# Layer 0 attention: scores of two heads in neighbouring PSUM banks thresholded by one instruction

## Chip, core and metric

The program runs on one core of a Trainium2 chip. The metric is the device time of one execution in microseconds (us). The core has five instruction streams: PE (TensorE, matmuls, with its weight loads listed as PEld), DVE (VectorE), ACT (ScalarE), POOL (GpSimd) and SP (SyncE, here only issuing DMAs). They meet only at semaphores. PSUM, where PE puts its results, has 8 banks of 512 fp32 columns in each of 128 partitions.

## What is computed

Two transformer layers over x of shape (2, 512, 256), each with an attention and a feed-forward part and a layer norm behind each. The change touches only the first attention, which has 16 heads of 16 channels and a threshold in place of the softmax:

```python
q, k, v = (proj(Wq), proj(Wk), proj(Wv))
scores = jnp.einsum('bhqd,bhkd->bhqk', q, k) * scale
w = jnp.where(causal, jax.nn.relu(scores - ATTN_THRESHOLD), 0.0)
w = w / (jnp.sum(w, axis=-1, keepdims=True) + EPS)
out = jnp.einsum('bhqk,bhkd->bhqd', w, v)
```

ATTN_THRESHOLD is -0.1, so every score s becomes max(s + 0.1, 0). Behind it stand layer 0's feed-forward part with Hadamard transforms, layer 1's attention with 32 query heads and a sliding window, and its feed-forward part.

## The kernel before

Everything is written out by hand: for each engine there is a list of steps (TENSOR_FIRST, SCALAR_FIRST, VECTOR_FIRST, GPSIMD_FIRST for layer 0's attention and what overlaps it), and an engine runs its steps in the order of its list. No planner decides anything, and the change leaves all lists alone.

For each of the two batches b, layer 0's 16 heads are taken in four groups hg of four heads (h4 = 0 to 3). The scores are kept transposed (128 keys in the partitions, queries in the columns), and since the mask is causal a block kb of keys needs only the queries from kb*128 on: 512, 384, 256 and 128 columns for kb = 0 to 3. A step `scores0(b, hg, part)` makes one part: part 0 is key block 0 (512 columns per head), part 1 is block 1 (384), part 2 is blocks 2 and 3 side by side (256 + 128 = 384). That is 2 x 4 x 3 = 24 steps. In each of them PE (line L553) writes four heads at the same time, each from 32 rows of the array, into four PSUM banks. Then ACT (L901) thresholds heads 0 and 2 and DVE (L1072) heads 1 and 3, one instruction per head, from PSUM into `weights_t`. POOL (L1339) waits until all four are done and zeroes the triangle of each key block with one `affine_select`. PE then multiplies by v in `pv0(b, hg, half_)` (L571; half 0 takes blocks 0 and 1, half 1 blocks 2 and 3), into bank 6. ACT copies the sums out (L911), PE turns them (L582, `turn0`, bank 7), and DVE divides (L1079 to L1081).

Six of the eight banks form a ring (RING = 6). `claim` hands out the next bank, and PE waits until the last user of that bank has emptied it: `pe.wait_ge(emptied_[bank], fills[bank])`. A `scores0` step claims four banks before its first matmul, so with six banks the next `scores0` step gets the two banks left over and the first two of the step before, when nothing else has claimed in between. The other steps that claim from the ring in this phase (`qk0`, `v0`, `at0`, `wo0`, `xt`, `prep_ug`, `prep_down`, `up`) take two banks each, so a `scores0` step always begins at an even bank.

A consumer calls `take`, which waits for the bank's `full` semaphore and returns the bank's `emptied` semaphore, to be raised by its instruction. PE's program holds an instruction's last wait in the instruction itself; the others stand ahead of it as instructions that only wait, with up to two conditions each.

## Time and profile before

| | |
|---|---|
| median of 3 runs | 520.43 us (520.12 to 520.55) |
| the profiled execution: device time | 520.81 us |
| its span, first to last instruction | 519.1 us |
| PE, DVE, ACT, POOL busy, share of the span | 92%, 74%, 65%, 46% |
| layer 0's attention, from the first scores to the last `turn0` | about 15 to 96 us |
| granted TensorE clock, mean over the span | 0.983 |

The profile is of one execution. Its page gives busy times, a line of 40 slices, the chain of work that ended last and the costliest groups; the trace behind it answers for single stretches. "Idle before <- X" names what ended an engine's idle time; a row marked x2 merges two instructions that follow each other, and its duration runs from the start of the first to the end of the second. "issue" is time in which an engine waited for nothing that the profile shows. Instructions that only wait are not listed as rows and show up as such "issue" time.

### The profile page before, as it was taken

How to read it: one execution, taken by the hardware profiler on the slowest of the kernel's cores; microseconds unless marked ns; L12 is line 12 of the kernel's file. 1: busy time of each engine (PE TensorE's matmuls, PEld its weight loads, DVE VectorE, ACT ScalarE, POOL GpSimd, SP SyncE). 2: the span in 40 equal slices, each digit the busy share in tenths (PEclk: the TensorE clock that was granted, in tenths of full speed). 3: DMA queues.
4: the chain of work that ended last, by engine and by line, in shares of the span. 5: the costliest groups of instructions: out<-in, count | busy, mean ns of one | idle time of the engine just before them, and what ended most of it. 6: DMA issues, size and time to landing. Idle time of an engine off the chain costs nothing.

```text
span 519.1 us, 10798 instructions
## 1 busy us (share of the span) xinstructions
PE 475.5 (92%) x3848; PEld 399.3 (77%) x3848; DVE 384.5 (74%) x675; ACT 335.8 (65%) x940; POOL 240.5 (46%) x167
## 2 busy tenths in 40 slices
PE   2799997999999977999999999998998699999995
PEld 1454653688888976799999999987997688889884
DVE  4455597778563689899899989999998975553534
ACT  3555564725534357998898988877988799333230
POOL 0377536321432477457656655656358821320001
PEclk9999997999999988999999999999999999999998
DMA  8500010023321000000000000001001312100101
GB/s 272 180 15 3 3 42 0 1 91 78 115 73 42 1 1 1 3 20 21 23 20 23 23 5 18 23 20 42 3 21 42 87 38 63 42 0 1 35 7 42
DMA packets 8612, 19.97 MB, mean 38 GB/s; under 512 B 1392, under 2 KB 2928, under 8 KB 8432
## 3 DMA queue, kind: packets, MB, share of 16 engines
q1 hardware_dynamic: 8560, 19.29, 11.8%
q8 instruction: 32, 0.52, 0.4%
q14 instruction: 20, 0.16, 0.1%
HBM read 18.23 MB, written 1.05 MB: 37 GB/s over the span
## 4 chain that ended last, share of the span: by engine, by line
PE 77%; DVE 11%; ACT 5%; issue 4%; DMA 1%; POOL 0%; DVEq 0%; POOLq 0%; SPq 0%; ACTq 0%
PE psum L499 17%; PE psum L501 16%; PE psum L500 15%; PE psum L553 5%; PE psum L725 4%; PE psum L715 4%; PE psum L737 4%; PE psum L571 4%; PE psum L696 3%; ACT probs L977 3%; DVE minus_max L1253 2%; PE psum L705 2%; DVE roped L1238 1%; DVE square_sums L1215 1%; DMA raw_chunks<-in_w 1%
## 5 line engine op out<-in xcount | busy, mean ns | idle before, releaser
L977 ACT ACTIVATE probs<-psum,minus_max 128x128 f32<-128x128 f32 x256 | 92.0, 399 | 16.0 <-issue 8.1
L1372 POOL TENSOR_TENSOR rope_sin_part<-qkv_rows,sin_weighted 128x640 f32<-128x640 f32 x32 | 51.2, 1623 | 48.6 <-DVE rope_cos_part L1222 42.3
L1381 POOL TENSOR_TENSOR rms_inverse<-rms_inverse,minus_half 128x20 f32<-128x20 f32 x16 | 63.5, 3970 | 1.3
L977 ACT ACTIVATION_READ_ACCUMULATOR probs<-psum,minus_max 128x1 f32 x256 | 60.7, 237 | 0.0
L945 ACT CAST hidden_high<-hidden 128x512 fp32r<-128x512 f32 x32 | 19.9, 622 | 61.1 <-DVE hidden L1168 61.1
L1253 DVE TENSOR_REDUCE minus_max<-psum 128x4 f32<-128x512 f32 x64 | 42.0, 685 | 14.6 <-PE psum L715 13.6
L499 PE MATMUL psum<-x_t_high,ug_high_low 128*128 128x512 f32 x128 | 51.1, 399 | 0.0
L501 PE MATMUL psum<-x_t_high,ug_high_low 128*128 128x512 f32 x128 | 50.7, 396 | 0.0
L500 PE MATMUL psum<-x_t_low,ug_high_low 128*128 128x512 f32 x128 | 50.5, 395 | 0.0
L499 PE MATMUL psum<-qkv_high_low,x_t_high 128*128 128x384 f32 x128 | 47.1, 368 | 3.1 <-ACT qkv_rows L950 1.7
L1247 DVE TENSOR_TENSOR probs<-probs,prob_inverse 128x512 f32<-128x512 f32 x64 | 48.0, 750 | 2.2
L950 ACT COPY qkv_rows<-psum 128x384 f32<-128x384 f32 x64 | 31.9, 511 | 18.4 <-PE psum L501 17.7
L500 PE MATMUL psum<-qkv_high_low,x_t_high 128*128 128x384 f32 x128 | 43.5, 340 | 0.0
L501 PE MATMUL psum<-qkv_high_low,x_t_low 128*128 128x384 f32 x128 | 43.4, 339 | 0.0
L1072 DVE TENSOR_SCALAR weights_t<-psum 128x384 f32<-128x384 f32 (+1 forms) x48 | 26.6, 596 | 21.2 <-PE psum L553 21.2
L901 ACT ACTIVATE weights_t<-psum,bias_threshold 128x384 f32<-128x384 f32 (+1 forms) x48 | 27.0, 616 | 22.0 <-PE psum L553 22.0
L499 PE MATMUL psum<-wout_high,out_t_high 128*128 128x256 f32 x128 | 38.7, 303 | 0.5 <-DVE out_t_low L1033 0.5
L1339 POOL TENSOR_SCALAR_AFFINE_SELECT weights_t<-weights_t 128x512 f32<-128x512 f32 x32 | 21.8, 696 | 36.8 <-DVE weights_t L1072 20.7
L1171 DVE TENSOR_TENSOR hidden_low<-hidden,hidden_high 128x512 fp32r<-128x512 f32 x32 | 22.2, 694 | 22.0 <-ACT hidden_high L945 22.0
L987 ACT COPY probs_t<-psum 128x512 f32<-128x512 f32 x64 | 37.4, 626 | 0.5 <-PE psum L725 0.3
L725 PE MATMUL psum<-identity,probs 128*128 128x128 f32 x256 | 36.2, 275 | 1.4 <-ACT probs L977 1.2
L499 PE MATMUL psum<-down_high_low,hidden_high 128*128 128x256 f32 x128 | 36.4, 284 | 0.5 <-issue 0.5
(145 smaller groups left out, 1381.4 us busy)
## 6 DMA issues: line engine op xcount, KB each, us to landing
raw_chunks<-in_ug SPq DMA_DIRECT2D x8, 512.0 KB, 3.9
raw_chunks<-in_wout SPq DMA_DIRECT2D x16, 256.0 KB, 2.8
raw_chunks<-in_qkv SPq DMA_DIRECT2D x8, 384.0 KB, 3.2
raw_chunks<-in_x SPq DMA_DIRECT2D x2, 512.0 KB, 4.6
raw_chunks<-in_w SPq DMA_DIRECT2D x2, 512.0 KB, 6.5
down_tree<-in_down SPq DMA_DIRECT2D x1, 1024.0 KB, 8.5
x_rows<-in_x_rows SPq DMA_DIRECT2D x2, 512.0 KB, 4.9
raw_chunks<-in_down SPq DMA_DIRECT2D x2, 512.0 KB, 3.9
```

What stands on the lines that cost most here:

```text
L499: nc.tensor.matmul(o, ah_, bh_, start=first, stop=False, **kw)
L500: nc.tensor.matmul(o, ah_, bl_, start=False, stop=False, **kw)
L501: return nc.tensor.matmul(o, al_, bh_, start=False, stop=last, **kw)
L725: mm = nc.tensor.transpose(o[:, q * P:(q + 1) * P], pr[:, c, q, :], ident[:])
L901: nc.scalar.activation(wt[:, hg % 2, h4, at:at + w], o[:, 0:w], ACT.Relu, bias=bias0[:]).then_inc(done, 1)
L950: nc.scalar.copy(qraw[:, k % 2, t, :], o[:, 0:GV]).then_inc(done, 1)
L977: e = nc.scalar.activation(pr[:, c, q, :], o[:, q * P:(q + 1) * P], ACT.Exp, bias=negm[:, c, q:q + 1], accum_out=psum1[:, c, q:q + 1])
L987: nc.scalar.copy(prt[:, c, :], o).then_inc(done, 1)
L1247: nc.vector.tensor_tensor(pr[:, c], pr[:, c], pinv[:, c, :].rearrange("p (q a) -> p q a", a=1).to_broadcast([P, 4, P]), ALU.mult).then_inc ...
L1253: nc.vector.tensor_reduce(negm[:, c, :], o.rearrange("p (q w) -> p q w", q=4), AX.X, ALU.max, negate=True).then_inc(mx_done[c], 1)
L1372: last = nc.gpsimd.tensor_tensor(ov[:, :, :, z, :], rv[:, :, :, 1 - z, :], sv[:, :, :, z, :], ALU.mult)
L1381: nc.gpsimd.tensor_tensor(r, r, half[:], ALU.pow).then_inc(rr_done, 1)
```

## The change

The 24 `scores0` steps claim their four banks as two pairs of neighbouring banks (0 and 1, 2 and 3, 4 and 5). A pair has a `pair_full` semaphore, raised once by each of its two heads (so the consumer waits for 2n + 2), and a `pair_emptied` semaphore, raised once by its one consumer. ACT thresholds the pair of heads 0 and 1 in one instruction over `[128, 2, w]`, DVE the pair of heads 2 and 3. POOL waits for two pair semaphores in place of four bank semaphores. Every bank now has two histories, fills as a single bank and fills as part of a pair, so every `claim` of a ring bank, up to the end of the program, waits for both. The banks that each step gets are the same as before.

```diff
@@ claim @@
                 if fills[bank]:
                     pe.wait_ge(emptied_[bank], fills[bank])
+                if bank < RING and pair_fills[bank // 2]:
+                    pe.wait_ge(pair_emptied[bank // 2], pair_fills[bank // 2])
...
+            def claim_pair(key):
+
+                if ring_at[0] % 2:
+                    ring_at[0] += 1
+                bank = ring_at[0] % RING
+                ring_at[0] += 2
+                job[key] = (bank // 2, pair_fills[bank // 2])
+                for b in (bank, bank + 1):
+                    if fills[b]:
+                        pe.wait_ge(emptied_[b], fills[b])
+                if pair_fills[bank // 2]:
+                    pe.wait_ge(pair_emptied[bank // 2], pair_fills[bank // 2])
+                pair_fills[bank // 2] += 1
+                return bank, pair_full[bank // 2]
...
-                heads = [claim(("scores0", b, hg, part, h4)) for h4 in range(HG)]
+                heads = []
+                for pr in range(2):
+                    bank, done = claim_pair(("scores0", b, hg, part, pr))
+                    heads += [(ps[:, bank + h2, :], done) for h2 in range(2)]
...
+        def take_pair(eng, key):
+
+            pair_, n = job[key]
+            eng.wait_ge(pair_full[pair_], 2 * n + 2)
+            return ps[:, 2 * pair_:2 * pair_ + 2, :], pair_emptied[pair_]
...
-                for h4 in (0, 2):
-                    o, done = take(act, ("scores0", b, hg, part, h4))
-                    nc.scalar.activation(wt[:, hg % 2, h4, at:at + w], o[:, 0:w], ACT.Relu,
-                                         bias=bias0[:]).then_inc(done, 1)
+                o, done = take_pair(act, ("scores0", b, hg, part, 0))
+                nc.scalar.activation(wt[:, hg % 2, 0:2, at:at + w], o[:, :, 0:w], ACT.Relu,
+                                     bias=bias0[:]).then_inc(done, 1)
...
-                for h4 in (1, 3):
-                    o, done = take(dve, ("scores0", b, hg, part, h4))
-                    nc.vector.tensor_scalar(wt[:, hg % 2, h4, at:at + w], o[:, 0:w], -ATTN_THRESHOLD, 0.0,
-                                            ALU.add, ALU.max).then_inc(done, 1)
+                o, done = take_pair(dve, ("scores0", b, hg, part, 1))
+                nc.vector.tensor_scalar(wt[:, hg % 2, 2:4, at:at + w], o[:, :, 0:w], -ATTN_THRESHOLD, 0.0,
+                                        ALU.add, ALU.max).then_inc(done, 1)
...
-                emptied(pool, *[("scores0", b, hg, part, h4) for h4 in range(HG)])
+                for pr in range(2):
+                    pair_, n = job["scores0", b, hg, part, pr]
+                    pool.wait_ge(pair_emptied[pair_], n + 1)
```

What stands in a row on the engines, at three places. Line numbers of the changed kernel differ: L553 has become L576, L571 L594, L499 L504, L582 L605, L901 L935, L911 L945, L885 and L887 L920 and L922.

PE at `scores0(0, 1, 0)`, `scores0(0, 1, 1)` and the first matmul of `qk0(0, 1)`, before:

```order
L553 MATMUL psum<-q_t,k_t 128x512 [waits bank5_emptied,bank0_emptied,bank4_emptied,bank1_emptied]
L553 MATMUL psum<-q_t,k_t 128x512 x3
L553 MATMUL psum<-q_t,k_t 128x384 [waits bank4_emptied,bank5_emptied,bank3_emptied,bank2_emptied]
L553 MATMUL psum<-q_t,k_t 128x384 x3
L499 MATMUL psum<-x_t_high,w_high 128x512 [waits chunk_low_dve,chunk_high,bank0_emptied]
```

The same place in the changed kernel:

```order
L576 MATMUL psum<-q_t,k_t 128x512 [waits bank0_emptied,bank1_emptied,banks45_emptied,banks01_emptied]
L576 MATMUL psum<-q_t,k_t 128x512 x3
L576 MATMUL psum<-q_t,k_t 128x384 [waits banks45_emptied,banks23_emptied]
L576 MATMUL psum<-q_t,k_t 128x384 x3
L504 MATMUL psum<-x_t_high,w_high 128x512 [waits chunk_low_dve,bank0_emptied,chunk_high,banks01_emptied]
```

No matmul has moved. The second step waited for four banks, of which 4 and 5 are heads 0 and 1 of the step right ahead; now it waits for the two pairs.

PE from `scores0(0, 1, 2)` over `pv0(0, 0, 1)` to `scores0(0, 2, 0)` and `turn0(0, 0)`, before:

```order
L553 MATMUL psum<-q_t,k_t 128x256 [waits bank4_emptied,bank5_emptied,bank3_emptied,bank2_emptied]
L553 MATMUL psum<-q_t,k_t 128x256 x3
L553 MATMUL psum<-q_t,k_t 128x128 x4
L571 MATMUL psum<-weights_t,v_and_ones 32x256 [waits weights0_masked]
L571 MATMUL psum<-weights_t,v_and_ones 32x256 x3
L571 MATMUL psum<-weights_t,v_and_ones 32x128 [waits weights0_masked]
L571 MATMUL psum<-weights_t,v_and_ones 32x128 x3
L553 MATMUL psum<-q_t,k_t 128x512 [waits bank1_emptied,bank2_emptied,bank0_emptied,bank3_emptied]
L553 MATMUL psum<-q_t,k_t 128x512 x3
L582 MATMUL psum<-identity,out_t 128x128 [waits in_identity,bank6_emptied]
```

The same place in the changed kernel:

```order
L576 MATMUL psum<-q_t,k_t 128x256 [waits banks45_emptied,banks23_emptied]
L576 MATMUL psum<-q_t,k_t 128x256 x3
L576 MATMUL psum<-q_t,k_t 128x128 x4
L594 MATMUL psum<-weights_t,v_and_ones 32x256 [waits weights0_masked]
L594 MATMUL psum<-weights_t,v_and_ones 32x256 x3
L594 MATMUL psum<-weights_t,v_and_ones 32x128 [waits weights0_masked]
L594 MATMUL psum<-weights_t,v_and_ones 32x128 x3
L576 MATMUL psum<-q_t,k_t 128x512 [waits bank1_emptied,banks01_emptied,bank0_emptied,banks23_emptied]
L576 MATMUL psum<-q_t,k_t 128x512 x3
L605 MATMUL psum<-identity,out_t 128x128 [waits in_identity,bank6_emptied]
```

Again only the waits differ: where the step waited for banks 2 and 3 apart (heads 0 and 1 of the step ahead), it waits for the pair.

ACT over the same stretch, before, with its two thresholds per step:

```order
L901 ACTIVATE weights_t<-psum,bias_threshold 128x512 [waits bank4_full,bias_set]
L901 ACTIVATE weights_t<-psum,bias_threshold 128x512 [waits bank0_full]
L901 ACTIVATE weights_t<-psum,bias_threshold 128x384 [waits bank2_full,bias_set]
L901 ACTIVATE weights_t<-psum,bias_threshold 128x384 [waits bank4_full]
L885 ACTIVATE k_t<-psum,head_parity 128x512 [waits bank0_full,in_parity]
L887 ACTIVATE q_t<-psum 128x512 [waits bank1_full]
L901 ACTIVATE weights_t<-psum,bias_threshold 128x384 [waits bank2_full,bias_set]
L901 ACTIVATE weights_t<-psum,bias_threshold 128x384 [waits bank4_full]
L911 COPY out_t<-psum 128x512 [waits bank6_full]
```

And in the changed kernel:

```order
L935 ACTIVATE weights_t<-psum,bias_threshold 128x2x512 [waits banks45_full,bias_set]
L935 ACTIVATE weights_t<-psum,bias_threshold 128x2x384 [waits banks23_full,bias_set]
L920 ACTIVATE k_t<-psum,head_parity 128x512 [waits bank0_full,in_parity]
L922 ACTIVATE q_t<-psum 128x512 [waits bank1_full]
L935 ACTIVATE weights_t<-psum,bias_threshold 128x2x384 [waits banks23_full,bias_set]
L945 COPY out_t<-psum 128x512 [waits bank6_full]
```

Two instructions of 512 or 384 columns have become one of twice as many, and nothing else on ACT has moved. DVE looks alike, with heads 2 and 3.

## Rows read from the trace of the kernel before

**Rows 1.** The page: its first line, and busy time by engine.
```profile
span 519.1 us, 10798 instructions
PE 475.5 (92%) x3848; PEld 399.3 (77%) x3848; DVE 384.5 (74%) x675; ACT 335.8 (65%) x940; POOL 240.5 (46%) x167
```
**Rows 2.** Stretches: us, busy PE, PEld, DVE, ACT, POOL (instructions), granted clock, DMA share, GB/s.
```profile
20.00:50.00 30.00, 27.41 (x276) 13.71 (x272) 16.66 (x32) 17.55 (x32) 20.39 (x20) 1.00 0.11 35
...
225.00:335.00 110.00, 110.00 (x1046) 100.56 (x1046) 100.28 (x161) 97.24 (x336) 67.62 (x37) 1.00 0.06 18
...
82.00:85.00 3.00, 0.00 (x0) 0.00 (x0) 3.00 (x8) 1.73 (x4) 1.20 (x1) 1.00 0.00 0
85.00:92.00 7.00, 6.80 (x36) 4.56 (x37) 5.18 (x13) 4.20 (x7) 5.72 (x7) 0.51 0.00 0
```
**Rows 3.** Groups by shape: line, instruction, count, busy us, mean ns, idle before, releasers.
```profile
L901 ACT ACTIVATE weights_t<-psum,bias_threshold 128x384 f32<-128x384 f32 x32 | 16.9, 581 | 11.7 <-PE psum L553 11.7
L901 ACT ACTIVATE weights_t<-psum,bias_threshold 128x512 f32<-128x512 f32 x16 | 10.1, 685 | 10.2 <-PE psum L553 10.2
L877 ACT CAST qkv_high_low<-raw_chunks 128x768 fp32r<-128x768 f32 x8 | 6.7, 832 | 0.0
L877 ACT CAST prep_high<-ug_sum_difference 128x1024 fp32r<-128x1024 f32 x4 | 4.2, 1054 | 0.0
...
L1072 DVE TENSOR_SCALAR weights_t<-psum 128x384 f32<-128x384 f32 x32 | 16.3, 552 | 11.4 <-PE psum L553 11.4
L1072 DVE TENSOR_SCALAR weights_t<-psum 128x512 f32<-128x512 f32 x16 | 10.3, 685 | 9.8 <-PE psum L553 9.8
```
**Rows 4.** The chain of waits, 24.8 to 26 us: start us, us, what.
```profile
24.91 0.70 ACT weights_t L901
25.61 0.24 issue
25.85 0.56 PE psum L553
```
**Rows 5.** Timeline at `scores0(0, 2, 0)`: start us, us, engine, line, instruction, [idle before].
```profile
30.72 1.05 ACT L901 ACTIVATE weights_t<-psum,bias_threshold 128x384 f32<-128x384 f32 x2 [0.31 <-PE psum L553]
31.55 1.14 PE L553 MATMUL psum<-q_t,k_t 32*128 32x512 f32 x8
```
**Rows 6.** Timeline at the first and the last of the alike places, `scores0(0, 0, 2)` and `scores0(1, 1, 2)`.
```profile
20.35 1.05 ACT L901 ACTIVATE weights_t<-psum,bias_threshold 128x384 f32<-128x384 f32 x2 [0.31 <-PE psum L553]
21.18 0.94 PE L553 MATMUL psum<-q_t,k_t 32*128 32x256 f32 x16 [0.91 <-ACT weights_t L901]
...
62.73 1.05 ACT L901 ACTIVATE weights_t<-psum,bias_threshold 128x384 f32<-128x384 f32 x2 [1.82 <-PE psum L553]
63.56 0.71 PE L553 MATMUL psum<-q_t,k_t 32*128 32x256 f32 x8
```
**Rows 7.** Timeline at the last two `scores0` steps, 83.7 to 88 us.
```profile
83.77 1.28 DVE L1072 TENSOR_SCALAR weights_t<-psum 128x512 f32<-128x512 f32 x2
85.19 1.61 PE L553 MATMUL psum<-q_t,k_t 32*128 32x384 f32 x5 [3.22 <-DVE weights_t L1072]
...
86.91 1.05 ACT L901 ACTIVATE weights_t<-psum,bias_threshold 128x384 f32<-128x384 f32 x2 [0.97 <-PE psum L553]
87.83 1.67 PE L553 MATMUL psum<-q_t,k_t 32*128 32x256 f32 x16
```
**Rows 8.** PE behind POOL's masks: total of such idle time; two rows at 80 us.
```profile
  POOL weights_t L1339: 2.0, 5
...
80.21 1.28 POOL L1339 TENSOR_SCALAR_AFFINE_SELECT weights_t<-weights_t 128x512 f32<-128x512 f32 x2
...
81.55 0.16 PEld L571 LDWEIGHTS psum<-weights_t,v_and_ones 128*32 128x32 f32 x8 [0.48 <-POOL weights_t L1339]
```
**Rows 9.** PE's waits from 95 us on, largest and smallest group: total us, times, longest.
```profile
PE psum L696 <- DVE roped L1238: 2.9, 1, 2.9
...
PE psum L499 <- ACT probs_t L987: 0.4, 1, 0.4
```

More of the change, by code:

```diff
@@ L414, in post_ln_two_layers @@
         emptied_ = [sem(f"bank{i}_emptied") for i in range(8)]
+        pair_full = [sem(f"banks{2 * i}{2 * i + 1}_full") for i in range(RING // 2)]
+        pair_emptied = [sem(f"banks{2 * i}{2 * i + 1}_emptied") for i in range(RING // 2)]
         ch_in = [sem(f"chunk_in{i}") for i in range(SLOTS)]
@@ L450, in post_ln_two_layers @@
         fills = [0] * 8
+        pair_fills = [0] * (RING // 2)
         ring_at = [0]
@@ L783, in take, with pair_filled @@
             return ps[:, bank, :], emptied_[bank]
+        def pair_filled(eng, key):
+            pair_, n = job[key]
+            eng.wait_ge(pair_full[pair_], 2 * n + 2)
+        def take_pair(eng, key):
+            pair_, n = job[key]
+            eng.wait_ge(pair_full[pair_], 2 * n + 2)
+            return ps[:, 2 * pair_:2 * pair_ + 2, :], pair_emptied[pair_]
         def filled(eng, key):
@@ L881, in qk0 @@
                 if b:
-                    filled(act, ("scores0", b - 1, 2 * m + 1, 2, HG - 1))
+                    for pr in range(2):
+                        pair_filled(act, ("scores0", b - 1, 2 * m + 1, 2, pr))
                 o, _ = take(act, ("qk0", b, 1, m))
@@ L1062, in qk0 @@
                 if b:
-                    filled(dve, ("scores0", b - 1, 2 * m + 1, 2, HG - 1))
+                    for pr in range(2):
+                        pair_filled(dve, ("scores0", b - 1, 2 * m + 1, 2, pr))
                 o, done = take(dve, ("qk0", b, 1, m))
@@ L1334, in scores0 @@
             def scores0(b, hg, part):
-                emptied(pool, *[("scores0", b, hg, part, h4) for h4 in range(HG)])
+                for pr in range(2):
+                    pair_, n = job["scores0", b, hg, part, pr]
+                    pool.wait_ge(pair_emptied[pair_], n + 1)
                 for kb in PART_BLOCKS[part]:
```

## Prediction, made before the changed kernel ran

> **What bounds the kernel now.** I first read the page's busy times: PE has work for 92% of the span, no other engine for more than 74% [rows 1]. Then the stretches: from 20 to 50 us PE is busy 27.41 of 30 us, while DVE and ACT are busy little more than half of it (16.66 and 17.55), and from 225 to 335 us PE is busy without a gap [rows 2]. There is one hole, 82 to 85 us, in which PE does nothing and DVE works through [rows 2]. So in the part that the change touches the two engines that are relieved are not the bound; what counts is when they let PE go on. The groups by shape say the same: before the thresholds ACT sat idle for 11.7 + 10.2 us and DVE for 11.4 + 9.8 us, all of it waiting for the scores [rows 3]. A faster threshold is worth something only where PE waits for it.
>
> Then I looked at who PE waits for, with the chain of waits and the timeline. At 25.61 us ACT ends its first threshold of `scores0(0, 1, 0)`, and 0.24 us later PE starts `scores0(0, 1, 1)` [rows 4]. At 30.72 us ACT starts the two thresholds of `scores0(0, 1, 2)`; the first lasts 0.58 us [rows 3], ends at 31.30, and PE starts `scores0(0, 2, 0)` at 31.55, again 0.25 us later, while ACT is still busy with the second until 31.77 [rows 5]. The same sum fits at 20.35 + 0.58 + 0.25 = 21.18 and 62.73 + 0.58 + 0.25 = 63.56 [rows 6]. A distance that is the same to 0.01 us at every such place, whatever PE did in between, means that the release by ACT's **first** instruction sets PE's start. I find it seven times: PE's starts at 21.18, 31.55, 40.36, 44.92, 46.73 and 63.56 us (first and last in [rows 6]) behind a part of 384 columns, and 25.85 us behind one of 512. They are the places where a `scores0` step follows the one before with nothing, with `turn0` or with the short second half of `pv0` in between. Where `qk0`, `v0` or the long first half of `pv0` stand in between, PE is itself the later one.
>
> **Part 1: the pair is released later than its first head was.** Each of the seven waits for heads 0 and 1 of the step before. They were freed by the first instruction of ACT and the first of DVE. Now both are ACT's pair, freed when 768 or 1024 columns are through. The trace of before has no such instruction from PSUM, so I bound it. The slope of ACT's thresholds is 685 - 581 = 104 ns for 128 columns [rows 3], 0.81 ns a column, which gives 581 + 384 x 0.81 = 892 ns for 768 columns and 685 + 512 x 0.81 = 1100 ns for 1024. From below: a cast of 768 columns from SBUF took 832 ns, one of 1024 took 1054 ns [rows 3]. From above: the two instructions together took 1.05 us, 0.11 us less than their sum [rows 3, 5], which makes 2 x 0.685 - 0.11 = 1.26 us for two of 512 columns. I take 0.90 and 1.10 us, by the slope of the same instruction. So the release comes 0.90 - 0.58 = 0.32 us later (0.25 to 0.47), and in the 512 case 1.10 - 0.69 = 0.41 us (0.37 to 0.57).
>
> **Part 2: waits on PE.** Of the 0.24 us between release and start [rows 4], two instructions that only wait and the matmul's own wait take part. Where PE is let go by a wait in the instruction itself it takes less: POOL's second mask ends at 80.21 + 1.28 = 81.49 and the weight load behind it starts at 81.55, 0.06 us later [rows 8]. So one wait instruction costs (0.24 - 0.06) / 2 = 0.09 us when it stands behind the last release. In the changed kernel the pair's wait stands last but for the matmul's own at all seven places, so one of the two falls out of this stretch: -0.09 us each (0 to -0.18).
>
> The two together: six places x (0.32 - 0.09) = 1.38 us, and one x (0.41 - 0.09) = 0.32 us, 1.7 us in all. With the lower ends (0.16 and 0.28) it is 1.2 us, with the upper ends (0.38 and 0.48) 2.8 us. PE is the bound around these places [rows 2], so nothing catches the loss up: the next matmuls, and with them all thresholds, start later by it.
>
> **Part 3: the two last steps.** At 85.19 PE starts `scores0(1, 3, 1)`, which needs all four banks of the step before, when DVE's second threshold is through at 85.05 [rows 7]. DVE's pair of 1024 columns costs 685 + 512 x 1.04 (133 ns for 128 columns) = 1.22 us, against 1.28 now: -0.06 us. One more step waits for DVE's last head in this way, behind 384 columns: about -0.05. At 87.83 PE starts the last `scores0` step [rows 7]. ACT's first threshold ended at 87.49 (86.91 + 0.58 [rows 7]), 0.34 us earlier, so PE itself (`turn0` at half clock) was the later one. Now ACT's pair ends at 86.91 + 0.90 = 87.81, and with 0.15 us to start PE is at 87.96: +0.13. Part 3 is 0.
>
> **Part 4: the thresholds' end, and POOL.** The step's last bank is emptied 0.05 to 0.15 us earlier than now, and POOL has half the waits. This helps where PE waits for a mask; such idle time is 2.0 us in five places [rows 8]. The largest of them, at 80 to 81.5 us, is POOL's own queue (the layer norm's power stands ahead of the masks), and PE's wait for DVE until 85.05 swallows what is won there. I put it at 0 (0 to -0.5 us), hidden under PE's own work.
>
> The Trainium skill speaks for a gain here. Its page "VectorE: DVE Perf Modes", in the section on the TRN2 errata, says that a fixed latency is paid per instruction, so that "a single large tile pays it once; many small tiles pay it per-tile". The rows agree in kind but not in amount: the two instructions of a step overlap (1.05 us for two of 0.58), so 0.15 us (1.05 - 0.90) is left to win rather than the 0.25 us of one fixed part; and by the rule alone 24 steps x 0.25 us = 6 us would go off ACT, which ACT spends waiting for PE.
>
> **Part 5: the rest of the program.** Every later claim of a ring bank has one more wait on PE, already satisfied. In the built programs PE has 204 wait instructions more, some 135 of them behind 99 us. From 225 to 335 us PE has many waits in its program and still no gap [rows 2], so waits that are satisfied run ahead of the array and cost nothing there. They cost 0.09 us only where PE has just been let go. From 95 us on, PE's idle time has 23 such ends (the largest and the smallest group in [rows 9]), 12 of them at lines whose claims got a wait more (L499, L705, L619): 0 to 1.1 us. I take 0.3 us, as the added wait mostly stands ahead of the one that comes last.
>
> The skill's page "Advanced Engine Details and Errata", section "Sequencer Loop", says that other engine instructions can be read and queued while a control instruction executes. By it all 204 are free and part 5 would be 0. The gapless stretch agrees; the 0.24 us of the chain shows that it ends where the queue has run dry.
>
> **The sum.** 1.7 + 0 + 0 + 0.3 = +2.0 us. The profiled execution took 520.81 us (span 519.1), so the like of it would take 522.8 us; it lies 0.38 us above the median of the runs, 520.43, and on that median the forecast is **522.4 us**. Its own range is 521.6 (+1.2 and nothing from part 5, or 1.7 less the 0.5 us of part 4) to 524.3 us (+2.8 and +1.1).
>
> **Rivals.**
>
> A. The loss is taken back later. All seven places lie before 64 us. Should PE's later idle time (3.2 us before 85.19 [rows 7], others behind 190 us) be ended by something that does not hang on PE, a DMA or POOL's own queue, the delay is eaten by it. Against it: the hole at 82 us is ended by a DVE that is busy 3.00 of 3 us [rows 2], behind layer norm sums that need PE's `wo0`, so it moves along with PE. The time would be 520.43 + 0.3 (part 5) = 520.7 us. Chance 0.22.
>
> B. It ends on the other side, because the end of a step counts and not its first release. Price: at the nine places where PE waits for a whole step (four) or for a mask (five, [rows 8]) it gains 0.15 + 0.09 us, 2.2 us; and with the pair at its lower bound (0.83 us) the seven places cost only 7 x 0.16 = 1.1 us. That gives 519.3 us; the page named in part 4 points this way. It decides from the point where the pair takes under 0.85 us and the mask waits are on the path. Against it: the seven distances of 0.25 us, and that only 2.0 us of mask waits exist. Chance 0.14.
>
> C. The clock. After the hole of 82 to 85 us the granted clock was 0.51 for 7 us [rows 2], the lower of TensorE's two levels (1.2 GHz) nearly all the time, which costs some 3.4 us. All gaps grow a little; one more such stretch of half that length would add 1.7 us: 524.1 us. Nothing in the rows says that it must come. Chance 0.08.
>
> That the change does not do what it says I give no chance: the program order shows one instruction per pair and the same banks as before.
>
> **Numbers.** The forecast has the chance 0.56. A measurement of this kernel tells about 0.2% (1.04 us) from no change. Slower by more: forecast and C, 0.64. Within: A, 0.22. Faster: B, 0.14. The range, 520.0 to 524.3 us, holds the forecast's own range, C, and A down to 0.4 us under the median, and leaves out B and a tail.
>
> **What the profile after would show.** ACT's pair at 0.90 us for 384 columns and 1.10 for 512 (DVE 0.95 and 1.22); the distance from ACT's release to PE's start at the seven places 0.15 us; PE's start of `scores0(0, 0, 2)` at about 21.4 and the last `turn0` of the phase about 1.7 us later than before; PE gapless from about 227 to 337 us. The forecast is wrong if the pair takes under 0.75 us, if PE's start at the seven places doesn't follow ACT's pair, if the delay is there at 64 us and gone at 190, or if gaps appear at claims in the gapless stretch, which would make 204 waits dear (0.09 x 204 = 18 us at the very most).

## The result and the profile after

The changed kernel takes 523.54 us (median of 4 executions, 522.49 to 523.82) where the kernel before takes 520.49 us: a ratio of 1.0055, 95% interval 1.0038 to 1.0072. Two further series gave 1.0060 (1.0040 to 1.0079) and 1.0057 (1.0037 to 1.0078). It is slower, by about 3.0 us; the forecast was 2.0 us, in a range that reached 3.9.

The page of the kernel after, its first line and busy times, to be read against [rows 1]:

```profile
span 520.8 us, 10934 instructions
PE 475.5 (91%) x3848; PEld 399.4 (77%) x3848; DVE 382.9 (74%) x651; ACT 332.1 (64%) x916; POOL 241.4 (46%) x167
```

ACT has 3.7 us less to do and DVE 1.6 us, with 24 instructions fewer each, and PE has exactly as much as before. The span is longer all the same. The groups by shape (line, instruction, count, busy us, mean ns, idle before) answer to [rows 3]:

```profile
L1106 DVE TENSOR_SCALAR weights_t<-psum 128x768 f32<-128x768 f32 x16 | 15.3, 956 | 12.7 <-PE psum L576 12.7
L935 ACT ACTIVATE weights_t<-psum,bias_threshold 128x768 f32<-128x768 f32 x16 | 14.4, 903 | 13.4 <-PE psum L576 13.4
L1106 DVE TENSOR_SCALAR weights_t<-psum 128x1024 f32<-128x1024 f32 x8 | 9.8, 1222 | 11.1 <-PE psum L576 11.1
L935 ACT ACTIVATE weights_t<-psum,bias_threshold 128x1024 f32<-128x1024 f32 x8 | 8.9, 1115 | 12.2 <-PE psum L576 12.2
```

The pair takes 0.90 and 1.12 us on ACT and 0.96 and 1.22 us on DVE. What ACT saved, 3.7 us here, has gone into its idle time: 21.9 us before the thresholds became 25.6, all waiting for PE's scores.

The windows answer to [rows 2] (us, busy PE, PEld, DVE, ACT, POOL with counts, granted clock, DMA share, GB/s):

```profile
20.00:50.00 30.00, 25.77 (x262) 13.18 (x260) 14.93 (x20) 14.98 (x20) 19.03 (x20) 1.00 0.12 35
...
225.00:335.00 110.00, 110.00 (x1050) 100.94 (x1048) 100.31 (x162) 97.45 (x336) 67.41 (x37) 1.00 0.07 18
```

Between 20 and 50 us PE lost 1.64 us of work (27.41 to 25.77). In the long stretch PE is without a gap, as before. The chain of waits of the kernel after, 20 to 27 us, shows the mechanism at the first two of the seven places, and answers to [rows 4]:

```profile
20.45 0.91 ACT weights_t L935
21.36 0.14 issue
21.50 0.94 PE psum L576 x16
22.43 1.64 PE psum L594 x16
24.07 1.11 PE psum L576 x6
...
25.27 1.12 ACT weights_t L935
26.39 0.14 issue
26.52 0.56 PE psum L576
```

ACT's whole pair now lies on the chain, and 0.14 us after it PE starts (before, 0.24 us after the first of two). The timeline has the same distances where [rows 5, 6] had theirs:

```profile
31.44 0.90 ACT L935 ACTIVATE weights_t<-psum,bias_threshold 128x768 f32<-128x768 f32 x1 [0.35 <-PE psum L576]
...
32.49 1.09 PE L576 MATMUL psum<-q_t,k_t 32*128 32x512 f32 x5 [0.38 <-ACT weights_t L935]
...
64.47 0.90 ACT L935 ACTIVATE weights_t<-psum,bias_threshold 128x768 f32<-128x768 f32 x1 [1.97 <-PE psum L576]
...
65.51 0.71 PE L576 MATMUL psum<-q_t,k_t 32*128 32x256 f32 x8 [0.38 <-ACT weights_t L935]
```

### Where the time went, matmul by matmul

PE's 3848 matmuls stand in the same order in every kernel here, so the start of each can be subtracted from the start of the same matmul in another trace (both counted from the first matmul). Between the traces of before and after this delay grows at the seven places of the prediction, by +0.26, +0.36, +0.26, +0.25, +0.25, +0.26 and +0.25 us, and between them by nothing: 1.89 us. That is the largest term. The rest lies behind 66 us, and a second trace of each kernel showed that much of it differs from one execution to the next.

### The profile page after: what moved, and what is told of

Read it like the earlier page. It is cut to its first block, busy times and chain, and to the rows that moved or that the text cites. A ratio compares the mean times of both kernels' runs of the same rounds, so it can differ in the third digit from the quotient of the medians.

```text
span 520.8 us, 10934 instructions
## 1 busy us (share of the span) xinstructions
PE 475.5 (91%) x3848; PEld 399.4 (77%) x3848; DVE 382.9 (74%) x651; ACT 332.1 (64%) x916; POOL 241.4 (46%) x167
## 3 DMA queue, kind: packets, MB, share of 16 engines
HBM read 18.23 MB, written 1.05 MB: 37 GB/s over the span
## 4 chain that ended last, share of the span: by engine, by line
PE 75%; DVE 12%; ACT 5%; issue 5%; POOL 1%; DMA 1%; DVEq 0%; POOLq 0%; SPq 0%; ACTq 0%
PE psum L504 16%; PE psum L506 15%; PE psum L505 15%; PE psum L748 5%; PE psum L738 4%; PE psum L760 4%; PE psum L576 4%; PE psum L719 3%; PE psum L594 3%; DVE minus_max L1287 2%; ACT weights_t L935 2%; DVE roped L1272 2%; PE psum L728 2%; ACT probs L1011 1%; PE psum L711 1%
## 5 line engine op out<-in xcount | busy, mean ns | idle before, releaser
L1417 POOL TENSOR_TENSOR rms_inverse<-rms_inverse,minus_half 128x20 f32<-128x20 f32 x16 | 64.6, 4040 | 1.3
L504 PE MATMUL psum<-x_t_high,ug_high_low 128*128 128x512 f32 x128 | 51.1, 399 | 0.0
L504 PE MATMUL psum<-qkv_high_low,x_t_high 128*128 128x384 f32 x128 | 46.9, 366 | 3.9 <-ACT qkv_rows L984 1.8
L1106 DVE TENSOR_SCALAR weights_t<-psum 128x768 f32<-128x768 f32 (+1 forms) x24 | 25.1, 1045 | 23.8 <-PE psum L576 23.8
L935 ACT ACTIVATE weights_t<-psum,bias_threshold 128x768 f32<-128x768 f32 (+1 forms) x24 | 23.4, 974 | 25.6 <-PE psum L576 25.6
L504 PE MATMUL psum<-wout_high,out_t_high 128*128 128x256 f32 x128 | 39.0, 305 | 0.5 <-DVE out_t_low L1067 0.5
L504 PE MATMUL psum<-down_high_low,hidden_high 128*128 128x256 f32 x128 | 36.4, 284 | 0.5 <-issue 0.5
```

Source lines behind the costliest of these rows:

```text
L504: nc.tensor.matmul(o, ah_, bh_, start=first, stop=False, **kw)
L935: nc.scalar.activation(wt[:, hg % 2, 0:2, at:at + w], o[:, :, 0:w], ACT.Relu, bias=bias0[:]).then_inc(done, 1)
L1417: nc.gpsimd.tensor_tensor(r, r, half[:], ALU.pow).then_inc(rr_done, 1)
```

## Experiments

All are edits of one of the two kernels. "Places" is the growth of the delay from 20 to 66 us, which holds the seven places and nothing else; "ratio" is to the kernel before on the same chip, with its interval. It compares all executions and not the two medians: the executions of most kernels here fall into two or more groups (below), and a median can jump from one to the other.

| kernel | places, us | median, us | ratio |
|---|---|---|---|
| the changed kernel, three series | +1.89, +1.87, +1.88 | 523.54, 523.60, 522.88 | 1.0055, 1.0060, 1.0057 |
| `two_instructions` | +2.95 | 525.30 | 1.0089 (1.0066 to 1.0112) |
| `pair_semaphores` | -0.49 | 519.39 | 0.9991 (0.9972 to 1.0010) |
| `last_user` | +1.88 | 522.87 | 1.0051 (1.0031 to 1.0071) |
| `last_user_first` | +1.26 | 521.73 | 1.0023 (1.0008 to 1.0039) |
| `whole_step` | +1.56 | 521.24 | 1.0036 (1.0018 to 1.0054) |
| `pair_semaphores_first`, two series | -1.00, -1.01 | 519.52, 519.08 | 0.9997, 0.9986 |
| `selective`, two series | -1.00, -1.01 | 518.59, 518.51 | 0.9971, 0.9974 |
| `before_again` | 0.00 | 520.30 | 0.9998 (0.9979 to 1.0017) |

### Is it the later release, or the added waits?

Theory L says that the loss is the pair's later release at seven places. Its rival W says that it is the 204 wait instructions that PE got. The first four runs shared a chip.

The changed kernel again:

> The changed kernel once more, for a second trace of it. Theory L (the pair's later release at seven places): the delay against the kernel before grows by 0.25 us at the same seven places (0.36 us where the step has 512 columns), about 1.9 us by 66 us, and the time is 523.5 us. What the time has beyond that (about 1.1 us) should then show behind 90 us in the trace, as a stretch at the lower clock or as gaps. Rival W (the 204 added wait instructions): the delay grows in many small steps all over the program, behind 99 us too, and is not the same at the seven places.

Measured: 523.60 us. The seven steps are there again to 0.02 us. As W wanted, there are also small steps further on, but they are few. The time beyond the places is where the expectation had it, behind 90 us, and in part at half clock (the table of delays below).

Two instructions per pair in place of one:

```diff
                 o, done = take_pair(act, ("scores0", b, hg, part, 0))
-                nc.scalar.activation(wt[:, hg % 2, 0:2, at:at + w], o[:, :, 0:w], ACT.Relu,
-                                     bias=bias0[:]).then_inc(done, 1)
+                for h2 in range(2):
+                    nc.scalar.activation(wt[:, hg % 2, h2, at:at + w], o[:, h2, 0:w], ACT.Relu,
+                                         bias=bias0[:]).then_inc(done, 1)
```

DVE likewise; the pair's semaphore counts two per use.

> The changed kernel with its pairs and their semaphores, but each pair is thresholded by two instructions of one head each instead of one instruction over both; the pair counts as emptied when both are through. Waits on PE are the same 204 more. Two overlapping instructions take 1.05 us where the pair took 0.90 (1.27 against 1.12 for 512 columns). Theory L: PE's start at the seven places comes 0.15 us later still, 7 x 0.15 = 1.05 us, 524.5 us. Rival W (added waits carry the loss): 523.5 us, the same as the changed kernel.

Measured: 525.30 us, and at the places +2.95 us, 1.06 us more than the changed kernel (expected 1.05). The timeline of this kernel at `scores0(0, 0, 2)`:

```profile
20.13 1.05 ACT L936 ACTIVATE weights_t<-psum,bias_threshold 128x384 f32<-128x384 f32 x2 [0.35 <-PE psum L576]
...
21.33 0.94 PE L576 MATMUL psum<-q_t,k_t 32*128 32x256 f32 x16 [1.32 <-ACT weights_t L936]
```

20.13 + 1.05 + 0.15 = 21.33: PE waits for the second instruction. With the waits unchanged, the time moved with the release, which W does not allow. (The median is 1.7 us above the changed kernel's, 0.8 above what was expected; the 0.6 us beyond the places are of the kind treated below.) It also shows that in this assignment of heads the one instruction is better than two; what costs is that heads 0 and 1 lie on one engine.

The waits alone, with the heads as before:

```diff
-                o, done = take_pair(act, ("scores0", b, hg, part, 0))
-                nc.scalar.activation(wt[:, hg % 2, 0:2, at:at + w], o[:, :, 0:w], ACT.Relu,
-                                     bias=bias0[:]).then_inc(done, 1)
+                for pr in range(2):
+                    o, done = take_pair(act, ("scores0", b, hg, part, pr))
+                    nc.scalar.activation(wt[:, hg % 2, 2 * pr, at:at + w], o[:, 0, 0:w], ACT.Relu,
+                                         bias=bias0[:]).then_inc(done, 1)
```

DVE takes head `2 * pr + 1`, and both raise the pair's semaphore.

> The pairs of banks, their semaphores and all 204 added wait instructions, but the thresholds as in the kernel before: ACT heads 0 and 2, DVE heads 1 and 3, one instruction each, so that heads 0 and 1 are free after 0.58 us again; ACT and DVE both raise the pair's semaphore. Theory L: the loss is gone; at the seven places PE is let go after 0.58 us and one wait instruction fewer stands behind the release, -7 x 0.09 = -0.6 us, and the added waits cost about 0.3 us: 520.1 us. Rival W: nearly all of the loss stays, 523 us or more.

Measured: 519.39 us, 0.7 under what was expected, and the loss is gone with all 204 waits in place. W falls as the main cause; what the waits do cost comes next. At the places the kernel gains 0.49 us, 0.07 each:

```profile
21.19 1.05 ACT L936 ACTIVATE weights_t<-psum,bias_threshold 128x384 f32<-128x384 f32 x2 [0.35 <-PE psum L576]
...
21.91 0.94 PE L576 MATMUL psum<-q_t,k_t 32*128 32x256 f32 x16 [0.85 <-ACT weights_t L936]
```

21.19 + 0.58 + 0.14 = 21.91: the first instruction lets PE go again, and 0.14 us of waits stand behind it, not 0.25. Of the 0.10 us gained there, 0.04 are lost ahead: ACT's idle time before its first threshold is 0.35 us where it was 0.31 [rows 6], since it now waits until both heads of the pair are written.

### What the added waits cost

In `last_user` a claim waits only for the last user of the bank, the pair's semaphore or the bank's own, since the older one is implied (`claim_pair` is changed alike):

```diff
                 if fills[bank]:
-                    pe.wait_ge(emptied_[bank], fills[bank])
-                if bank < RING and pair_fills[bank // 2]:
-                    pe.wait_ge(pair_emptied[bank // 2], pair_fills[bank // 2])
+                if bank < RING and last_pair[bank]:
+                    pe.wait_ge(pair_emptied[bank // 2], pair_fills[bank // 2])
+                elif fills[bank]:
+                    pe.wait_ge(emptied_[bank], fills[bank])
```

> The changed kernel with one instruction per pair, but a claim waits only for the last user of the bank (the pair's semaphore or the bank's own, not both; the older one is implied by it). PE's program has 423 wait instructions instead of 650 (the kernel before has 446). Theory L: only part 5 of the prediction goes, -0.3 us, and perhaps 0.1 us where a wait fewer stands behind the release: 523.1 us. Rival W: the loss goes with the waits, 520.5 us.

Measured: 522.87 us, 0.73 under the changed kernel on that chip, with the same +1.88 at the places. The two traces differ by 0.70 us where they can be compared: 0.20 between 66 and 85 us, and 0.50 behind 110 us. The largest single step is 0.26 us at the first matmul of a feed-forward step (0.11 us in the first and the third trace of the changed kernel). PE's rows there, the changed kernel in its second trace:

```profile
119.67 1.03 PE L633 MATMUL psum<-identity,x_rows 128*128 128x128 f32 x8
120.84 0.19 PEld L504 LDWEIGHTS psum<-x_t_high,ug_high_low 128*128 128x128 f32 x1 [0.38 <-issue]
120.88 0.47 PE L504 MATMUL psum<-x_t_high,ug_high_low 128*128 128x512 f32 x1 [0.17 <-issue]
```

and `last_user` at the same matmul:

```profile
119.75 0.19 PEld L506 LDWEIGHTS psum<-x_t_high,ug_high_low 128*128 128x128 f32 x1
119.78 0.47 PE L506 MATMUL psum<-x_t_high,ug_high_low 128*128 128x512 f32 x1
```

Without the second wait there is no gap, and none of the kernels without it has the step, while all with it have 0.11 or 0.26 us. So a satisfied wait was free in the stretch without gaps (225 to 335 us), and cost up to 0.26 us at this boundary. The Trainium skill's page "Advanced Engine Details and Errata", section "Sequencer Loop", by which other instructions can be queued while a control instruction executes, fits the first stretch; at 120.9 us this trace shows a wait that was not hidden.

### The order of the waits

Of several waits PE's program holds one in the matmul itself (the last in its row of the order) and the others as instructions ahead of it. The one in the matmul turned out to be the call that is made first. `last_user_first` calls the wait that ends last first:

```diff
-                for pr in range(2):
-                    bank, done = claim_pair(("scores0", b, hg, part, pr))
+                for pr in range(2):
+                    bank, done = claim_pair(("scores0", b, hg, part, pr), waits)
...
+                for semaphore, value in reversed(waits):
+                    pe.wait_ge(semaphore, value)
```

> The kernel last_user with the same waits in another order: the wait for the pair that comes free last stands in the first matmul of the step itself, and the satisfied ones are the instructions ahead of it. One instruction fewer stands behind the release: 7 x 0.09 = 0.6 us less than last_user, 522.3 us; PE starts 0.06 us after ACT's pair. If a wait instruction behind the release costs nothing, the time stays 522.9 us.

Measured: +1.26 at the places where `last_user` had +1.88: 0.62 less, 0.09 each, as expected. The median is 521.73 us where 522.3 was expected, on another chip; its executions fall into 4 of 520.25 to 520.45 us and 8 of 521.59 to 522.23. Its timeline:

```profile
20.39 0.90 ACT L940 ACTIVATE weights_t<-psum,bias_threshold 128x768 f32<-128x768 f32 x1 [0.35 <-PE psum L581]
...
21.34 0.94 PE L581 MATMUL psum<-q_t,k_t 32*128 32x256 f32 x16 [1.07 <-ACT weights_t L940]
```

20.39 + 0.90 + 0.05 = 21.34. The distance from release to start is thus 0.05, 0.15 or 0.25 us with no, one or two wait instructions still to be passed after the release, ahead of the matmul.

### The rest: where the half clock falls

The table's ratios are larger than its places explain. Second traces were taken to see why.

> The kernel before once more, for a second trace of it: the stretches at half clock and the first matmuls can then be compared between two traces of one kernel. If the 3.1 to 3.5 us by which the changed kernel is slower come from the seven places alone (1.9 us), the rest must be chance: then a second trace of before has stretches at half clock of 13 to 14 us in sum, as the two traces of the changed kernel have. If the longer hole behind the late release keeps the clock down longer (rival C), this trace has clearly less, 11 us or under.

Measured: 520.30 us for the series. The traced execution took 518.52 us, that of the profile before 520.81. The expectation went by the sum of the stretches at half clock: 13 to 14 us would speak for chance, 11 or under for rival C. This trace has 3.4 us (without the last few us of the program, where every trace has one), the first trace of the same kernel 13.6, and the changed kernel's three traces 13.6 each. Since the sum moves by 10 us within one kernel, one trace decides nothing here. Windows of the second trace of before (columns as above):

```profile
82.00:85.00 3.00, 0.29 (x8) 0.02 (x4) 3.00 (x8) 1.41 (x3) 0.88 (x1) 1.00 0.00 0
86.00:89.00 3.00, 3.00 (x20) 1.58 (x16) 2.15 (x4) 1.31 (x3) 1.91 (x3) 0.50 0.00 0
90.00:92.00 2.00, 2.00 (x19) 1.39 (x21) 1.93 (x7) 2.00 (x5) 2.00 (x2) 1.00 0.00 0
191.00:194.00 3.00, 1.89 (x13) 1.36 (x11) 3.00 (x4) 3.00 (x6) 3.00 (x3) 1.00 0.00 0
205.00:207.00 2.00, 1.40 (x10) 1.13 (x9) 1.76 (x6) 2.00 (x11) 0.00 (x0) 1.00 0.03 8
```

Behind the hole at 82 us the clock is at its lower level (0.50, 1.2 GHz) until 89.1 us; in the first trace it stayed there until 91.9. And the first trace has two more such stretches, one of them here:

```profile
205.00:207.00 2.00, 2.00 (x11) 2.00 (x10) 1.91 (x7) 0.68 (x5) 0.33 (x1) 0.50 0.03 8
```

The changed kernel's trace has three as well:

```profile
89.00:95.00 6.00, 5.73 (x32) 4.39 (x36) 5.04 (x9) 3.30 (x6) 5.15 (x5) 0.50 0.00 0
195.00:197.00 2.00, 2.00 (x10) 2.00 (x9) 2.00 (x3) 2.00 (x3) 2.00 (x1) 0.50 0.00 0
410.00:412.00 2.00, 2.00 (x12) 2.00 (x10) 1.97 (x3) 2.00 (x5) 2.00 (x2) 0.50 0.00 0
```

The delay against the quiet trace, `before_again`, by part of the program (us; "start" is what the first 20 us differ by, the last column the whole):

| trace | start | places | 66-85 | 85-110 | 110-203 | 203-215 | 215-400 | 400-420 | behind | all |
|---|---|---|---|---|---|---|---|---|---|---|
| before | -0.27 | 0.00 | 0.00 | 1.56 | 0.01 | 1.03 | -0.01 | 0.01 | 0.01 | 2.34 |
| after, first | -0.18 | 1.89 | 0.13 | 1.86 | 0.07 | 0.00 | -0.06 | 0.11 | 0.22 | 4.04 |
| after, second | 0.40 | 1.87 | 0.13 | 0.99 | 0.21 | 0.00 | -0.04 | 1.37 | 0.16 | 5.10 |
| `two_instructions` | -0.54 | 2.95 | 0.19 | 1.64 | 0.30 | 0.00 | -0.04 | 1.49 | 0.16 | 6.16 |
| `last_user` | 0.11 | 1.88 | -0.07 | 0.82 | -0.01 | 0.00 | -0.17 | 1.42 | 0.01 | 3.98 |
| `whole_step` | -0.32 | 1.56 | 0.00 | 0.21 | -0.01 | 1.25 | -0.01 | 0.00 | 0.01 | 2.70 |

Every entry above 0.8 us outside "places" has a stretch at half clock in it that the quiet trace lacks, or has shorter. Such a stretch costs 1.0 to 1.6 us at 202 to 208 or at 410 to 419 us, where PE has no idle time behind it to give up, and nothing at 191 to 198 us or in the first trace of after at 409.5 us (which, since that trace runs 4 us late, is an earlier place in the program), where PE would have waited anyway. An execution gets none, one or more of the dear ones. In the pool of executions of before that went with `before_again`, 15 of 35 took 518.2 to 518.7 us and the others 520.1 us or more. Of the 18 executions of the changed kernel none lies near 518.5 + 1.9 us; the lowest is 521.89.

The mean granted clock of every execution is on record too, and tells how much of it ran at half clock. In the 94 executions of the kernel before that went with the experiments it is 0.983 to 0.993, and 0.988 or more in 50 of them; the 32 that took under 519 us all have 0.989 or more. The 18 of the changed kernel all have 0.982 to 0.986. The averages are 0.9873 and 0.9848, so the changed kernel runs about 0.0025 x 520 x 2 = 2.6 us longer at half clock, three quarters of a stretch of 3.4 us.

Is that the pair's doing, or that of any delay ahead of the hole? `whole_step` is the kernel before, in which PE waits at four of the seven places for all four heads of the step ahead:

```diff
+                step_ahead = {(0, 0, 2): (0, 0, 1), (0, 2, 0): (0, 1, 2), (0, 3, 0): (0, 2, 2), (1, 1, 2): (1, 1, 1)}
+                if (b, hg, part) in step_ahead:
+                    emptied(pe, *[("scores0", *step_ahead[b, hg, part], h4) for h4 in (2, 3)])
                 heads = [claim(("scores0", b, hg, part, h4)) for h4 in range(HG)]
```

> The kernel before, with every instruction as it was, but at four of the seven places (PE's starts at 21.18, 31.55, 40.36 and 63.56 us) PE also waits for heads 2 and 3 of the step ahead, which are free 0.47 us after heads 0 and 1, with one wait instruction more (0.09 us): 4 x 0.56 = 2.2 us of delay, all of it before 64 us, about what the changed kernel loses at its seven places (1.9 us), without a pair and without the 204 waits. Theory L+C (a delay ahead of the hole at 82 us costs itself and something in the stretches at half clock): 523.5 us and no execution under 521.5 us. Theory L alone: the executions of the kernel before shifted by 2.2 us, two groups at 520.7 and 522.5 us. If the changed kernel's loss beyond 1.9 us comes from its pairs and waits, it is the second.

> The changed kernel beside whole_step on the same chip. The seven places cost 0.25 us each (0.36 the second) as in the two traces of it so far. If the delay moves where the stretches at half clock fall, its executions lie as those of whole_step do, 522 to 524 us; if its own waits matter, they lie up to 0.8 us above them.

Measured: the places are +1.56 us, not 2.2: 0.28, 0.53, 0.49 and 0.27 us. At the first and the last of the four the added wait call is the first one made, landed in the matmul itself and so cost nothing behind the release (PE starts 0.06 us behind ACT's second threshold). At the other two the wait for `qk0` is called ahead of it, and the steps are near the 0.56 that were expected.

The executions fall into two groups, 520.70 to 521.34 (7) and 522.17 to 523.38 us (5). So there are two groups, with middles of 521.0 and 522.9 us and executions under 521.5 us, as theory L alone had it, and not one late group. But since the delay came out at 1.56 us, the groups lie 0.9 and 0.7 us further up than it explains (middles of 518.5 and 520.6 us on the same chip for the kernel before). The changed kernel beside it took 521.89 to 524.06 us. The ratio is 0.36% above 1 (interval 0.18 to 0.54), which is 1.9 us. On the same chip the changed kernel was at 1.0057, 1.1 us more; its places account for 0.3 of these (1.88 - 1.56) and its waits for 0.7. So nothing has to be put down to the pairs as such.

The mean clock of `whole_step` is 0.9846, with 0.988 or more in one of 12 executions: more half clock than in the kernel before appears with a delay at the places and without any pair. But `selective` below, which is not delayed at the places, has 0.9860 and 0.9851 and is the fastest kernel: the delay is not the only cause of it, and its amount alone is not its cost. What the half clock adds beyond the delay itself, here up to 0.9 us in each group, isn't settled: I have no run that moves the stretches without moving the work.

### Is the paired instruction any good where nobody waits?

> The kernel pair_semaphores (thresholds as in the kernel before, one semaphore per pair raised by ACT and by DVE), with a claim waiting for the last user alone (423 wait instructions on PE), and the wait that ends last in the matmul itself. Theory L: 519.4 - 0.6 (seven places) - 0.2 (fewer waits) = 518.6 us, 1.4 to 1.9 us under the kernel before. If only the size of the instruction counts and not its waits, it stays at 519.4 us.

> The kernel pair_semaphores_first, with the change's one instruction per pair in the 16 steps behind which no scores0 step stands waiting, and one instruction per head in the other 8 (the seven places and one that is 0.09 us short of waiting). Theory L: where nobody waits for the first release, the paired instruction costs and gains nothing: the same time as pair_semaphores_first, 518.6 us. Rival B (the end of a step counts): the last bank of 16 steps is emptied up to 0.15 us earlier, which gives 0.5 to 1.5 us more, 517.1 to 518.1 us.

`pair_semaphores_first` is `pair_semaphores` with the edits of `last_user` and `last_user_first`. `selective` adds to it the change's one instruction per pair, but not in eight steps:

```diff
+        one_by_one = {(0, 0, 1), (0, 1, 0), (0, 1, 2), (0, 2, 2), (0, 3, 1), (0, 3, 2), (1, 1, 1), (1, 3, 1)}
...
+                if (b, hg, part) not in one_by_one:
+                    o, done = take_pair(act, ("scores0", b, hg, part, 0))
+                    nc.scalar.activation(wt[:, hg % 2, 0:2, at:at + w], o[:, :, 0:w], ACT.Relu,
+                                         bias=bias0[:]).then_inc(done, 1)
+                    return
```

Measured: 519.52 and 518.59 us, with the same 1.00 us gained at the places. 518.6 us were expected of both, so the first missed by 0.9 us: against the kernel before its ratio is 0.9997, and the 1.00 us doesn't show in it. The timeline of `pair_semaphores_first`:

```profile
21.06 1.05 ACT L941 ACTIVATE weights_t<-psum,bias_threshold 128x384 f32<-128x384 f32 x2 [0.36 <-PE psum L581]
...
21.69 0.94 PE L581 MATMUL psum<-q_t,k_t 32*128 32x256 f32 x16 [0.75 <-ACT weights_t L941]
```

21.06 + 0.58 + 0.05 = 21.69. Both ran once more, side by side:

> The kernel selective once more beside pair_semaphores_first, since their first medians (518.59 and 519.52 us) differ while their traces have gained the same 1.0 us at the seven places. If one instruction per pair in the 16 steps where nobody waits for the first release is worth something (rival B's gain), it is again 0.5 to 0.9 us below pair_semaphores_first. If it is worth nothing there, the two lie within 0.4 us of each other, both at 518.5 to 519.6 us.

> The kernel pair_semaphores_first beside selective_again on the same chip: 518.5 to 519.6 us, and PE's starts at the seven places 0.14 us earlier each than in the kernel before, 1.0 us in sum.

Measured: 518.51 us (0.9974, interval 0.9956 to 0.9992) and 519.08 us (0.9986, 0.9967 to 1.0006). `selective` is the fastest kernel of the study: it beats the kernel before in both series, and the changed kernel by 4 to 5 us in the median (on other chips).

It is ahead of `pair_semaphores_first` by 0.9 and 0.6 us, and by the measure set ahead of the second series (0.5 to 0.9 us again) that speaks for a gain from the paired instructions. It is still not shown: the intervals overlap, and the second traces of the two differ by 0.3 us between 110 and 203 us and otherwise mainly by where the half clock fell (203 to 215 us in the one, 400 to 420 in the other, 1.3 and 1.5 us). The 0.3 us may well be real: in both traces of `pair_semaphores_first` PE's weight load at 120.5 us (121.7 in the first trace) waits for DVE, which is late with `ug_high_low`, and in neither of `selective`:

```profile
120.50 0.19 PEld L506 LDWEIGHTS psum<-x_t_high,ug_high_low 128*128 128x128 f32 x1 [0.17 <-DVE ug_high_low L1181]
```

## Why the prediction was right, and where its sizes were off

**What bounds the kernel**: right. ACT and DVE lost work and turned it into idle time; the only thing that moved the end was when PE was let go.

**Part 1**: right. ACT's pair took 0.90 and 1.12 us (0.90 and 1.10 forecast), DVE's 0.96 and 1.22 (0.95 and 1.22).

**Part 2**: right. A wait instruction costs 0.10 us behind the release (0.09 forecast), and PE starts 0.15 us behind it. The seven places cost 1.89 us, not 1.7: the step lacked a term, that a consumer of a pair starts when both heads are written, 0.03 to 0.05 us later than for one.

**Part 3**: right at 0. At 85.19 us the delay falls by 0.07 us (0.06 forecast), at 68.8 us by 0.08 (0.05). At the last scores step it grows by 0.16 us (0.13) in the second trace of the changed kernel, where the same matmuls run at half clock as in the first trace of before; in the other two traces the clock differs there.

**Part 4**: right at 0. Idle time behind POOL's masks was 2.2 us in five places, as good as unchanged from [rows 8]. The passage of the Trainium skill quoted behind part 4 speaks of SBUF latency, and the thresholds read PSUM; for them the rows decide. ACT's pair took 0.15 us less than its two instructions, as forecast, and ACT spent the gain waiting for scores.

**Part 5** was too small. I took 0.3 us for the satisfied waits behind 99 us and nothing for those ahead of it; the runs show 0.5 and 0.2. I had counted a price of 0.09 us per wait and taken it that the queue hides most; at a single boundary it was 0.11 or 0.26. (The count of PE's waits from 95 us on missed one group of 0.3 us, at L499; it makes no difference.)

**From the profile to the median** was the step that failed in size. Corrected for the places (1.9 where I had 1.7) and the satisfied waits (0.7 where I had 0.3), the sum is 2.6 us, and 3.0 were measured. I carried the sum from the profiled execution to the median, as if the kernel's other costs stayed. The median of before is held down by its executions with little half clock, and the changed kernel had none of these in 18, `whole_step` one in 12 (mean clock of 0.988 or more). What that is worth was not measured by itself; 0.4 us are left for it, and the chance of the series.

**Rivals.** A (taken back later) is wrong: in the table of delays no part behind 66 us gives anything back to the changed kernel but 0.06 us between 215 and 400. B (the end of the step counts) is wrong at the seven places, by `pair_semaphores` and `two_instructions`. C asked for one more stretch at half clock, for 1.7 us. The first traces of before and after have three each, but by the mean clocks the changed kernel has 2.6 us more of it on average, three quarters of a stretch, so C is right in kind and wrong in price: about 0.4 us of the measured 3.0 are left for it.

## What to carry to other kernels

Before two instructions are merged, look at who waits for the first of them: here the consumer waited for half of the step, and merging across that half delayed it by about a quarter of a microsecond each time, for engines that had time to spare. Put the wait that ends last into the waiting instruction itself and drop waits that another one implies; with one semaphore per pair, that gave 1.0 us at the seven places, as much as half of what the merge lost, though by itself it did not show in the ratio of the whole (0.9997 and 0.9986, both intervals with 1 in them). And read a difference of 2 or 3 us from the starts of the same instructions in two traces of each kernel before explaining it, for a stretch at half clock in the wrong place is worth up to 1.6 us alone.

## What the runs showed of the hardware

- At the seven places PE's start follows the release by 0.05, 0.15 or 0.25 us, with zero, one or two wait instructions between (to about 0.01 us, in every kernel whose rows are shown).
- A satisfied wait between two groups of matmuls cost 0.26 us at 120.9 us in one trace of the changed kernel, 0.11 us in two others, and nothing in the stretch without gaps.
- Two thresholds of 384 columns in a row on ACT take 1.05 us, one of 768 takes 0.90; of 512 and 1024 columns, 1.27 and 1.12.
- TensorE's granted clock fell to 0.50 (1.2 GHz) around the time when PE took up work behind 3.1 to 3.2 us of idle time (0.1 us ahead of it in the first trace of before, 0.2 us behind in the second, up to 1.5 us ahead and 1.7 behind in other kernels), and stayed there for 6.8 us in the one execution and 3.4 in the other of the same kernel. The same drop also came near 191, 204 or 411 us in some executions and not in others. Its cost was between 0 and 1.6 us, by whether PE had idle time behind it.
